# Writing out the 58 turns of the last edge product of a two-layer graph kernel

## What is computed

```python
def _spmm(edge_index, edge_weight, x, n):
    dst, src = (edge_index[0], edge_index[1])
    msg = edge_weight[:, None] * x[src]
    return jax.ops.segment_sum(msg, dst, num_segments=n)

def _L1_gnn_ref(feature, edge_weight, weight, bias, edge_index, mode):
    feature = feature - jnp.mean(feature, axis=0, keepdims=True)
    std = jnp.std(feature, axis=0, ddof=1) + 0.0001
    feature = feature / std
    support = _spmm(edge_index, edge_weight, feature, feature.shape[0])
    output = support @ weight
    return output + bias

x = _layernorm(x + first_layer(x, ...), axis=-1)
x = _layernorm(x + _L1_gnn_ref(x, edge_weight, L1_gnn_weight, L1_gnn_bias, edge_index, 2), axis=-1)
```

## Time and profile before

| | |
|---|---|
| median of 3 runs | 4683.7 us (4644.42 to 4695.43) |
| profiled execution | 4704.91 us |
| its span | 4703.2 us |
| mean granted clock of PE, share of full | 0.798 |
| PE busy | 2861.5 us (61%) |
| DVE busy | 2088.6 us (44%) |
| ACT busy | 963.5 us (20%) |
| POOL busy | 2812.6 us (60%) |
| POOL's gathers of the last product (L457), 928 | 886.5 us |
| PE's matmuls of the last product (L980), 3712 | 672.8 us |
| DVE's hot matrices (L1691), 928 | 270.4 us |
| DVE's adds (L1701), 464 | 195.4 us |

### The profile page before, as it was taken

The page is one execution under the profiler, slowest core; times in us unless marked ns, Lnnn a source line. Parts: engine busy times, 40 slices in busy tenths (PEclk is TensorE's granted clock), DMA queues, the critical chain, the costliest instruction groups (busy, mean ns, idle before and its releaser), DMA issues. The chain is left out here.

```text
span 4703.2 us, 65453 instructions
## 1 busy us (share of the span) xinstructions
PE 2861.5 (61%) x13606; PEld 2202.0 (47%) x13606; DVE 2088.6 (44%) x5189; ACT 963.5 (20%) x2658; POOL 2812.6 (60%) x2802
## 2 busy tenths in 40 slices
PE   3665656666666566648888888955445444544446
PEld 2443544334434334347777776334444444444444
DVE  5676652222222222225555556963333334433336
ACT  1332222222222222213333333520000000000002
POOL 4886755655555555646665665865555656656551
PEclk8777777877777787869999999987776766767768
DMA  3444434544544454537777776432222322223232
GB/s 106 122 119 133 155 106 153 161 155 160 161 157 155 149 164 157 157 105 230 233 236 219 237 234 192 141 120 79 80 81 78 86 79 84 85 79 86 80 81 81
DMA packets 313502, 643.93 MB, mean 137 GB/s; under 512 B 57970, under 2 KB 123423, under 8 KB 313436
## 3 DMA queue, kind: packets, MB, share of 16 engines
q0 software_dynamic: 124416, 341.61, 23.2%
q1 hardware_dynamic: 186532, 298.30, 21.4%
q10 hardware_dynamic: 2488, 3.28, 0.2%
HBM read 486.27 MB, written 156.69 MB: 137 GB/s over the span
## 5 line engine op out<-in xcount | busy, mean ns | idle before, releaser
L457 POOL DMA_INDIRECT work<-x_table,stage x928 | 886.5, 955 | 616.7 <-DVE stage L1685 323.9
L457 POOL DMA_INDIRECT work<-in_x,stage x832 | 938.1, 1128 | 529.6 <-issue 288.0
L477 POOL DMA_INDIRECT messages<-work,stage x832 | 815.1, 980 | 595.7 <-ACT work L600 340.6
L980 PE MATMUL ps<-work 128*128 128x128 f32 x3712 | 672.8, 359 | 794.5 <-DVE work L1691 610.5
L980 PEld LDWEIGHTS ps<-work 128*128 128x128 f32 x3712 | 635.9, 267 | 866.1 <-issue 577.8
L869 PE MATMUL ps<-work 128*128 128x256 f32 x1664 | 505.6, 457 | 418.2 <-DVE work L1402 265.8
L762 PE MATMUL ps<-work 128*128 128x128 f32 x3328 | 515.0, 319 | 373.1 <-ACT work L552 187.2
L762 PEld LDWEIGHTS ps<-work 128*128 128x128 f32 x3328 | 484.7, 229 | 458.9 <-issue 245.1
L869 PEld LDWEIGHTS ps<-work 128*128 128x128 f32 x1664 | 366.4, 230 | 544.9 <-issue 366.2
L600 ACT ACTIVATE work<-ps,columns 128x256 f32<-128x256 f32 x832 | 325.7, 475 | 904.8 <-PE ps L869 475.6
L1701 DVE TENSOR_TENSOR node_a<-node_a,ps 128x256 f32 x464 | 195.4, 421 | 708.8 <-remote 456.1
(11 more groups left out here) (228 smaller groups left out, 2986.3 us busy)
## 6 DMA issues: line engine op xcount, KB each, us to landing
work<-messages SPq DMA_DIRECT2D x232, 520.0 KB
work<-place_row SPq DMA_DIRECT2D x208, 256.0 KB
work<-in_x SPq DMA_DIRECT2D x256, 128.0 KB
gate_rows<-work SPq DMA_DIRECT2D x49, 384.0 KB
columns<-gate_rows SPq DMA_DIRECT2D x49, 384.0 KB, 3.0
work<-x_table,stage POOLq DMA_INDIRECT x928
work<-in_x,stage POOLq DMA_INDIRECT x832
messages<-work,stage POOLq DMA_INDIRECT x832
```

The source lines that it names most:

```text
L457: nc.gpsimd.indirect_dma_start(out=big[:, s, j, 0:D], out_offset=None, in_=table, in_offset=bass.IndirectOffsetOnAxis(ap=stage[:, s, j:j + ...
L477: nc.gpsimd.indirect_dma_start(out=messages, out_offset=bass.IndirectOffsetOnAxis(ap=stage[:, s, j:j + 1], axis=0), in_=big[:, s, j, :], i ...
L980: last = nc.tensor.matmul(ps[4 + h][:, (2 * u + d) * P:(2 * u + d + 1) * P], big[:, s, j, d * P:(d + 1) * P], hot[:, h, j, :], start=j % 2 ...
```

## The change

The loops over the turns of the last product become Python loops that write every turn out, on POOL, DVE and PE, and the loop over the squares on ACT. Every wait has the value that the register would have had, every address is that of the turn, and the order of the instructions on every engine stays. The body of POOL's loop becomes a function, `gather_turn`, which the other stages' loops call with the loop's register as before. The flag `first` of PE's sum of squares, which had told the one written-out turn from those of the loop, now names that turn. The side work, the buffers and the semaphores are the same.

```diff
 @block.gpsimd
+            def gather_turn(table, tag, i):
+                for s in range(RING):
+
+                    pool.wait_ge(S[f"{tag}_staged"], RING * i + s + 1)
+                    pool.sem_inc(S["may"], 1)
+                    for j in range(CPG):
+                        nc.gpsimd.indirect_dma_start(
+                            out=big[:, s, j, 0:D], out_offset=None, in_=table,
+                            in_offset=bass.IndirectOffsetOnAxis(ap=stage[:, s, j:j + 1], axis=0)).then_inc(S[f"{tag}_rows{s}"], 16)
+
             def gather(table, tag, lo, hi):
                 with pool.Fori(lo, hi) as i:
-                    for s in range(RING):
...
+                    gather_turn(table, tag, i)
...
-            gather(x1_table, "second", 0, BACK_TURNS)
+            for i in range(BACK_TURNS):
+                gather_turn(x1_table, "second", i)
 @block.scalar
-            with act.Fori(0, FULL // 4) as i:
+            for i in range(0, FULL // 4):
                 for s in range(2):
                     square_pair(2 * i + s, s)
 @block.tensor
             def pairs(i, s):
                 if s % 2:
-                    pair_sum(2 * (i - SUMMED - 1) + s // 2, s // 2, first=isinstance(i, int) and s == 1)
+                    pair_sum(2 * (i - SUMMED - 1) + s // 2, s // 2, first=isinstance(i, int) and i == SUMMED + 1 and s == 1)
             second_turn(SUMMED + 1, pairs)
-            with pe.Fori(SUMMED + 2, SQUARED) as i:
+            for i in range(SUMMED + 2, SQUARED):
                 second_turn(i, pairs)
...
-            with pe.Fori(SQUARED + 4, BACK_TURNS) as i:
+            for i in range(SQUARED + 4, BACK_TURNS):
                 second_turn(i)
 @block.vector
-            with dve.Fori(1, SUMMED + 1) as i:
+            for i in range(1, SUMMED + 1):
                 second_turn(i)
...
-            with dve.Fori(SUMMED + 2, SQUARED) as i:
+            for i in range(SUMMED + 2, SQUARED):
...
-            with dve.Fori(SHIFTS, SHIFTS + FULL // 2) as i:
+            for i in range(SHIFTS, SHIFTS + FULL // 2):
                 now[0] = i
                 add_shift(2 * (i - SHIFTS), 2)
                 second_turn(i)
             add_shift(FULL, 1)
-            with dve.Fori(SHIFTS + FULL // 2, BACK_TURNS - 1) as i:
+            for i in range(SHIFTS + FULL // 2, BACK_TURNS - 1):
                 second_turn(i)
             second_turn(BACK_TURNS - 1, last=True)
```

## The result

The changed kernel takes 4661.2 us (median of 16 runs, 4638.08 to 4679.83), the kernel before 4684.3 in the same series. The medians differ by 23 us. The ratio of the runs is 0.9958, with a 95% interval of 0.9938 to 0.9977, which is 11 to 29 us. A second series of the same pair, on another chip, gave 0.9956 (0.9935 to 0.9978). So the change makes the kernel about 0.45% faster, inside the 1% that I had taken as no change, and by a third of the 64 us that I had forecast.

The account below looks back on a forecast made before the run. POOL's gathers and DVE's stage copy were taken to lock each other. The middle of 27 and 102 us, 64, off the profiled 4704.9 gave 4641; less 21.2 to the runs' median, 4620 us, range 4545 to 4700.

Parts of the forecast that it names:

- What bounds the kernel: Last product: POOL waits 323.9 us for DVE's stage copy, while DVE's add is let go 2.6 us after POOL runs dry.
- the true rate lies between, I take the middle, 64: Last product's 50 looped turns: gain between 27 us by POOL's count and 102 by DVE's, taken as 64.
- the sample: Turns 19 to 23, already written out on DVE before the change: 24.0 us a turn by DVE, 25.4 by POOL.
- The term in itself: DVE's loop costs in the last product: written-out code was to make turns about 1.1 us shorter, 64 us in all.
- The slow register instructions, read as DVE's own weakness: L1691: DVE's sequencer falls behind, register instructions of median 93 and longest 712 ns, 57.1 us of idle before looped columns.
- At no cost: Last product: register work and branches of POOL, PE and ACT, and some 70 added instruction packets, were booked at nothing.
- the sign that I gave for costly code: Gaps in front of L980 that no hot column explains would show that longer code costs time.
- (a): Last product: run of 12 gathers and 5.11 us gap untouched by DVE's registers; 4657 to 4675 us; chance 0.24 with (d).
- (b): Last product: much more gained, bare written-out turns of 21.8 us, 4472 us; chance 0.14.
- (c): Last product: slower, 70 exposed code fetches at 3.0 us each, 210 us less the 64, 4830 us; chance 0.14.
- (d): Last product: the change does nothing, the loops having been hidden; sized as (a), chance 0.24 together with it.
- The unnamed wait about as long as now: Sign of a right forecast: DVE's wait with no named releaser, in the last product, was not claimed to be removed.

Follow-up runs that it names:

- e4: The changed kernel, the last product fetching only the first two of each group's four rows: 4083.4 us against 4672.7 or 4773.6.
- e8: The changed kernel, SP issuing the last product's row transfers as plain ones from the table's first 512 rows, POOL none: 3907.3 us, before 4746.3, one run.
- e14: The changed kernel with a chained memset of 256 columns on POOL behind every gather issue of the last product: 4550.3 us, before 4672.7, one run.
- e15: The kernel before, with all its loops, fetching only the first two of each group's four rows in the last product: 4087.4 us, before 4672.7, one run.
- e13: The kernel before, only POOL written out, with a 3.7 us rest of POOL after every 8 issues: 4770.1 us, before 4672.7, one run.
- e18: The kernel before, only POOL written out, with a memset of 256 columns behind every issue: 4553.7 us, ratio 0.9717.
- e2: The kernel before with PE's, POOL's and ACT's loops written out and DVE's kept: 4743.3 us, ratio 0.9947.
- e3: The changed kernel with 8 row slots in place of 4 in the last product: 4734.7 us, ratio 0.9916.
- e17: The changed kernel with a small memset of 8 columns on POOL behind every gather issue: 4647.0 us, ratio 0.9906.

## Why the prediction was wrong

**What bounds the kernel: right.** POOL's gathers, its wait for the copy, and the late release of the add. The lock is there after the change as before, and e4, e8 and e14 show that it is what keeps the turn above 25 us: with half the gathers, with none by POOL, or with one in 1.44 us, the turn falls below 24.

**The step that failed is "the true rate lies between, I take the middle, 64".** DVE's count of the sample said 24.0 us a turn, POOL's 25.4. With the change a turn is on average 25.24 us by POOL's count and 25.23 by DVE's, and 23 us came where POOL's count had given 27 and DVE's 102. I had written the reason down myself: POOL's lead shrank inside the sample, and a shrinking lead can't go on. DVE's 24.0 and the lead's fall of 6.8 us in five turns, 1.36 a turn, make POOL's 25.4. The result shows that this fall belongs to turns 19 to 23 whatever the code: DVE's count of them is 23.6 with every turn written out. And in the looped turns 24 to 56 the lead had grown again, from 7.5 to 14.0 us, which made DVE's 25.8 too long by 0.2. So the truth didn't lie between the two counts; the middle took in the move of the lead as if it were a gain. The 27 us aren't exact either: the two profiles differ by 34, of which 14 in turns 24 to 56, where POOL's count had given 8. And the sample's 9.2 us a turn of unnamed wait, which I listed for the rival, stayed and became 10.7 (622.5 us in 58).

**The term in itself: right in size, wrong in place.** 1.08 us a turn is what the loops cost DVE in e15 against e4. In the kernel it was given back: 83 us of idle before columns went, 166 us more of unnamed wait came. DVE reached the wait earlier and then stood in it longer, and in the steady turns the release follows POOL's last issue by some 3 us (2.6 before). What stayed is one group more in most runs: 16 gathers by 25.2 us in place of 12 by 19.85.

**The slow register instructions, read as DVE's own weakness: wrong.** The longest of 712 ns and the 57.1 us go when POOL issues less densely (e13, e15, e18).

**At no cost: right.** POOL's, PE's and ACT's registers: e2's turns are as before. (POOL's loop had four plain register instructions, a fused one and a branch a turn, and not one of each; it made no difference.) The fetches: in the last product 73 instruction packets in place of 16, and the time before POOL's gathers with nothing named went down, 292.8 to 259.7 us. PE was idle before its products for 793.9 us where it had been 794.5, so the sign that I gave for costly code, new gaps there, is absent too. The part of the rule of the Trainium skill that I had noted as agreeing (Runtime: NRT & Kernel Launch, section Instruction fetch mechanics) holds for long straight code too.

**The rivals.** (a) had the size, 9 to 27 us, and not the pattern: it said cycles of 12 and 19.85 us, they are of 16 and 25.2. What stays of it is its sentence, that the gap is set by something DVE's registers don't touch. (b) is what e14 comes nearest to, and it takes another edit. (c) is out, and (d) as well, since the interval excludes a ratio of 1.

**What would show it.** No column behind 0.9 us of idle: right. More runs of 16: right, nearly all. Turns about 1.1 us shorter by both counts: 0.6. The unnamed wait about as long as now: wrong, it grew by 166 us, and I hadn't asked what DVE does with the time it is given.

## What to carry to other kernels

When an engine is let go by an event that another engine's progress sets, time saved ahead of the wait can become wait; price a saving by the rate of the engine that paces the stage (here POOL, first gather to first gather), and don't average it with the rate of one that is catching up. If counts come late beside a run of POOL's indirect DMAs, look at the interval between issues before anything else: 1.25 us apart they went with late counts of PE, 1.44 apart with few or none, and slowing POOL by 15% made the kernel 2.8% faster. This kernel may have more of it: in its earlier stages DVE waits another 246 and 572 us unnamed ahead of what it reads from PSUM (L1246 and L1394), and POOL's issues there mostly come every 1.25 to 1.26 us. Whether that is the same hold, and whether spacing helps there, wasn't tried.

## What the runs showed of the hardware

- PE's count of a product came up to 33 us after its recorded end while POOL issued 36 indirect DMAs at 1.25 us each, and 2.2 us after the last (3.1 in the steady turns). Counts of DVE and of the DMAs came through meanwhile.
- At 1.25 us it begins some 10 us into a run (e3): with 8 issues and a rest of 3.7 us no count was over 2 us late; with a rest of 1.4 us 106 of 232 were.
- At one issue in 1.44 us, over 104 gathers without a pause of 1 us, none was (e14), or 13 were, late in these stretches (e18, with DVE in loops); at one in 1.26 us 97 were (e17).
- With plain DMAs of the same bytes, issued by SP, no count was over 1 us late (e8).
- Instructions of DVE's sequencer of 0.6 us and more in looped code come and go with the same condition: 215 of over 0.6 us before, 2 with rests, 4 with spacing, none with half the gathers. Counted in the trace, from the first gather of the last product on.
